# Four source tiles instead of two come row by row at register addresses

## The chip, the cores and the metric

The kernel runs on one core of a Trainium2 chip. The metric is the time of one execution on the device, in microseconds (us). Engines are named as in the profile: PE is TensorE (matmuls), DVE is VectorE, ACT is ScalarE, POOL is GpSimd and SP is SyncE. An engine's instruction queue issues DMAs in order with its other instructions; "ACTq" and "SPq" in a row are such issues.

## The reference

Two graph layers with a residual and a layer norm each, over 3125 nodes of 128 features and 53125 edges that are sorted by destination. Every edge needs the row of x of its source node.

```python
def layer0(h, src, dst, etype, norm, weight, w_comp, bias):
    hsrc, coef = h[src], w_comp[etype]
    msg = sum(hsrc @ weight[b] * coef[:, b][:, None] for b in range(8)) * norm
    return relu(segment_sum(msg, dst, num_segments=h.shape[0]) + bias)

def layer1(node, edge, src, dst, eps, W1, b1, gamma, beta, W2, b2):
    neigh = segment_sum(node[src] + edge, dst, num_segments=node.shape[0])
    h = ((1.0 + eps[0]) * node + neigh) @ W1 + b1
    h = (h - h.mean(0)) * rsqrt(h.var(0) + 1e-5) * gamma + beta
    return relu(h) @ W2 + b2

x = layernorm(x + layer0(x, src, dst, edge_type, edge_weight, ...))
out = layernorm(x + layer1(x, edge_attr, src, dst, ...))
```

## The kernel before

The edges are cut into 416 tiles of 128. Two tiles make a unit (208 units, U), four units a group (52, GROUPS), two units a couple. The main loop goes over the units. For each tile PE multiplies the 128 source rows of x with a one-hot matrix of the destinations that is weighted with the edge's coefficients, and DVE adds the windows that come out into `sums`. As the edges are sorted, the sums of low nodes are complete early; seven parts of the nodes (LOOPED) are therefore finished inside the loop: PE multiplies a part with the bases (line 1339), ACT keeps the result (`keep_agg`, line 1030), PE turns it, DVE makes the layer norm's statistics, ACT takes the deviations (`chunk_deviations`, line 1044), PE turns the normed rows and ACT copies them (`keep_x1_columns`, line 1052). The second layer's neighbour sums run on finished parts as "runs" between the units (line 1374). All of that is an order written out by hand: each engine goes through its own list of units and does a step at the unit where it stands, and semaphores tie the lists together.

The source rows come in three ways.

- POOL gathers a tile with one indirect DMA (`gather_unit`, line 921), up to 16 units ahead of PE (22 early on): 413 tiles.
- SP brings tile 414 (`load_rows_of_tile`, lines 803 to 810). In each of its steps from 23 on (a step is a group) it loads five node numbers from memory into registers (line 805) and issues one DMA of one row of 512 bytes for each (line 809). The five rows of the last tile, 415, it brings in the same way near the end (line 791).
- ACT brings tile 413 (`load_scalar_rows`, lines 1067 to 1074). From unit 152 on, it loads three numbers a unit (line 1069) and issues three row DMAs (line 1073). From there on ACT has no copies of counts left to do (line 1016), but the steps `keep_agg`, `chunk_deviations` and `keep_x1_columns` of the last parts stand between these rows in its queue.

The rows of SP and ACT land in `sums[:, 0, ...]`, in columns of parts whose sums are no longer needed. PE waits for a gathered tile by `gather_in`, for SP's rows by `rows_in` and for ACT's by `etype_rows_in`, in the unit that reads them:

```python
if u * UNIT < ROWED:
    pe.wait_ge(gather_in[u % RU], landed(u))
else:
    pe.wait_ge(rows_in, 16 * (6 + P + FRESH))
if (u + 1) * UNIT == ROWED:
    pe.wait_ge(etype_rows_in, 16 * (5 + P))
```

After unit 207 come the late bases (line 1348), the last runs and the dense layers, and SP stores the output. `late_bases(0)` stands behind unit 202 and waits for the last copy of `keep_x1_columns` (`x1_kept`).

Of the kernel before, what the change touches and what calls it, by code (L numbers as in the profile page):

```python
# [8 lines left out]
I32 = mybir.dt.int32  # L9
# [6 lines left out]
P = 128  # L16
# [5 lines left out]
UNIT = 2  # L22
# [4 lines left out]
ROW_STEP = 22  # L27
ROWS_EACH = 5
SCALAR_UNIT = 152
SCALAR_EACH = 3  # L30
PAIR = 2
# [11 lines left out]
def gnn_resnorm_kernel(nc, x, src, dst, edge_attr, etype, norm, weight, w_comp, bias0,  # L43
# [11 lines left out]
    N, F = x.shape  # L55
# [6 lines left out]
    T = -(-E // P)  # L62
# [51 lines left out]
    TWINS = 3  # L114
    ROWED = T - 2
    assert ROWED * P + P + FRESH == E and ROWED % UNIT == 0
    COUNT_FASTER = 2 * RING * GROUP
# [164 lines left out]
    with ExitStack() as ctx:  # L282
# [89 lines left out]

        row_place, row_sources = sums[:, 0, 0:F], sums[0:1, 0, F:2 * F].bitcast(I32)

        scalar_place, scalar_sources = sums[:, 0, 2 * F:3 * F], sums[0:1, 0, 3 * F:4 * F].bitcast(I32)

        def gathered_tile(t):

            if ROWED <= t < T - 1:
                return row_place  # L380
            if t == ROWED - 1:
                return scalar_place
            first = RING * GROUP
            if first <= t < first + SPARE:
                return sums[:, 0, SPARE_AT + (t - first) * F:SPARE_AT + (t - first + 1) * F]
            return gathered[:, (t if t < first else t - SPARE) % first, :]
# [290 lines left out]
        def landed(u):  # L677

            return (u // RU + 1) * 16 * UNIT - (16 if (u + 1) * UNIT == ROWED else 0)

# [11 lines left out]
        def _(sp):  # L692
# [32 lines left out]
            with sp.If(wide < 1):  # L725
# [73 lines left out]
                def load_row_sources():  # L799
                    sp.wait_ge(st_var, PART_AT[2])  # L800
                    sp.dma_start(row_sources, src[ROWED * P:ROWED * P + P].rearrange("(t e) -> t e", t=1)).then_inc(rows_in, 16)

                def load_rows_of_tile(first, last):
                    sp.wait_ge(rows_in, 16 * 6)
                    rows = nc.values_load_multi_w_load_instructions(
                        row_sources[:, first:last], engines=(ENGINE.SP,), min_val=0, max_val=N - 1,
                        skip_runtime_bounds_check_because="sources are node numbers")[1]
                    for i, row in enumerate(rows):
                        sp.dma_start(row_place[first + i:first + i + 1, :],
                                     x[bass.ds(row, 1), :]).then_inc(rows_in, 16)  # L810

                load_attrs(0)
                load_attrs(1)
                for g in range(GROUPS):
# [10 lines left out]
                    if g == ROW_STEP:  # L825
                        load_row_sources()
                    if 0 <= (g - ROW_STEP - 1) * ROWS_EACH < P:
                        at = (g - ROW_STEP - 1) * ROWS_EACH
                        load_rows_of_tile(at, min(P, at + ROWS_EACH))
                    if g == GROUPS - 3:  # L830
                        load_last_rows()
                load_late_rows_of_x()
                sp.wait_ge(gather_in[(U - 2) % RU], landed(U - 2))
                for b in LOAD_ORDER[12:13] + LOAD_ORDER[6:12]:
# [53 lines left out]
        def _(pool):  # L888
# [19 lines left out]
            def gather_unit(u):  # L908
# [5 lines left out]
                for t in range(u * UNIT, (u + 1) * UNIT):  # L914
                    if u >= FLYING + RU:
                        pool.wait_ge(tiles_read, t - RU * UNIT + 1)
                    elif u >= FLYING:
                        pool.wait_ge(tiles_read, t - FLYING * UNIT + 1)
                    if t + 1 >= ROWED:
                        continue  # L920
                    pool.indirect_dma_start(  # L921
                        gathered_tile(t), None, x[:, :],
                        bass.IndirectOffsetOnAxis((src_slots if t < AHEAD else src_i)[:, t:t + 1], 0)).then_inc(gather_in[u % RU], 16)
# [30 lines left out]
        def _(act):  # L954
# [106 lines left out]
            def load_scalar_sources():  # L1061

                first = (ROWED - 1) * P
                act.dma_start(scalar_sources, src[first:first + P].rearrange("(t e) -> t e", t=1)).then_inc(etype_rows_in, 16)

            def load_scalar_rows(first, last):
# [4 lines left out]
                    skip_runtime_bounds_check_because="sources are node numbers")[1]  # L1071
                for i, row in enumerate(rows):
                    act.dma_start(scalar_place[first + i:first + i + 1, :],
                                  x[bass.ds(row, 1), :]).then_inc(etype_rows_in, 16)

            places = [None] * GU
            with act.If(wide < 1):
# [4 lines left out]
                for u in range(U):  # L1082
# [6 lines left out]
                    if u == SCALAR_UNIT - 4:  # L1089
                        load_scalar_sources()  # L1090
                    if 0 <= (u - SCALAR_UNIT) * SCALAR_EACH < P:
                        at = (u - SCALAR_UNIT) * SCALAR_EACH
                        load_scalar_rows(at, min(P, at + SCALAR_EACH))
                    for k in range(LOOPED):
# [94 lines left out]
        def _(pe):  # L1189
# [74 lines left out]
            def narrow_sums():  # L1264
# [46 lines left out]
                def products_of_step(u):  # L1311
# [4 lines left out]
                    if counts:  # L1316
                        twin_product(counts[0])
                        count_product(counts[0], 0)
                    if u * UNIT < ROWED:
                        pe.wait_ge(gather_in[u % RU], landed(u))  # L1320
                    else:
                        pe.wait_ge(rows_in, 16 * (6 + P + FRESH))
                    if (u + 1) * UNIT == ROWED:
                        pe.wait_ge(etype_rows_in, 16 * (5 + P))
                    for i in range(UNIT):
# [805 lines left out]
```

## Time and profile before

| | us |
|---|---|
| median of 3 runs | 592.95 (591.94 to 595.67) |
| profiled execution, its own time | 591.92 |
| its span, from first to last instruction | 590.1 |
| PE busy | 499.6 |
| DVE busy | 464.3 |
| POOL busy | 399.0 |
| ACT busy | 220.3 |

Busy time counts an engine's work on data. The issue of a DMA, a load of registers and a wait on a semaphore are not in it, so a queue can be full while its engine's share is low. "Idle before" of a group of instructions is the time in which the engine did nothing ahead of them, and the arrow names what ended it. The granted clock is TensorE's, as a share of 2.4 GHz.

### The profile page before, as it was taken

The numbers are of one execution on the slowest core, as the hardware profiler recorded it, in microseconds if no ns is written. First come the engines' busy times: TensorE is split into PE (matmuls) and PEld (weight loads), VectorE is DVE, ScalarE is ACT, GpSimd is POOL, SyncE is SP. The second block draws the span as 40 slices with busy tenths as digits, with TensorE's granted clock in tenths as the row PEclk, the third lists the DMA queues.
The fourth block names the chain that finished last, engine by engine and source line by source line (L and its number), as shares of the span: only waits on it lengthen the run. The fifth ranks groups of instructions, "written<-read, shape, count | busy, mean of one in ns | idle before, by whom it ended". The sixth has DMA issues, their size and how long they took to land. (4 is left out here: it accounts for less than half of the span.)

```text
span 590.1 us, 13829 instructions
## 1 busy us (share of the span) xinstructions
PE 499.6 (85%) x3981; PEld 422.8 (72%) x3981; DVE 464.3 (79%) x1835; ACT 220.3 (37%) x325; POOL 399.0 (68%) x431
## 2 busy tenths in 40 slices
PE   3679887997977977878986888988999797798995
PEld 2458787876866766757575676677989787797675
DVE  5999999989998699989789888895554655655476
ACT  8914446445343264434354442430000000003386
POOL 7777777777777777777777777777777777750000
PEclk9987779597687898989889999999999978989999
DMA  5423757565676395667675775887575765743003
GB/s 142 126 51 90 249 186 220 174 200 180 201 242 238 87 308 161 217 216 245 206 228 189 227 258 189 269 278 226 182 243 141 230 197 154 227 121 119 2 1 109
DMA packets 103807, 108.18 MB, mean 183 GB/s; under 512 B 11726, under 2 KB 90822, under 8 KB 103730
## 3 DMA queue, kind: packets, MB, share of 16 engines
q1 hardware_dynamic: 84286, 77.88, 40.5%
q0 software_dynamic: 13216, 27.09, 17.1%
q10 hardware_dynamic: 6228, 2.30, 1.5%
q8 instruction: 34, 0.56, 0.4%
q14 instruction: 43, 0.35, 0.2%
HBM read 81.67 MB, written 25.56 MB: 182 GB/s over the span
## 5 line engine op out<-in xcount | busy, mean ns | idle before, releaser
L921 POOL DMA_INDIRECT gathered_flat<-in_x_dram,src_i x399 | 382.8, 959 | 121.6 <-issue 89.3
L1016 ACT ACTIVATE adj_flat<-psum 128x500 f16<-128x500 f32 (+1 forms) x208 | 127.4, 612 | 193.1 <-PE psum L1302 185.4
L1278 PE MATMUL psum<-weighted,gathered_flat 128*128 128x96 f32 (+1 forms) x804 | 142.8, 305 | 27.1 <-DMA gathered_flat<-in_x_dram,src_i 27.0
L1271 PEld LDWEIGHTS psum<-hot,attrs 128*128 128x128 f32 x832 | 146.5, 214 | 12.4 <-issue 9.7
L1278 PEld LDWEIGHTS psum<-weighted,gathered_flat 128*128 128x128 f32 x804 | 122.3, 213 | 30.9 <-DMA gathered_flat<-in_x_dram,src_i 30.7
L1782 DVE TENSOR_SCALAR etype_hot<-iota_key,key_t 128x300 f16<-128x300 f16 (+1 forms) x416 | 135.3, 327 | 0.0
L1271 PE MATMUL psum<-hot,attrs 128*128 128x12 f32 (+1 forms) x832 | 132.4, 236 | 2.4 <-DVE weighted L1663 2.4
L1302 PE MATMUL psum<-etype_hot 128*128 128x300 f16 (+1 forms) x416 | 128.0, 345 | 3.4 <-DVE etype_hot L1782 3.3
L1779 DVE TENSOR_SCALAR etype_hot<-iota_key,gathered_flat 128x128 f16<-128x128 f16 x416 | 106.8, 257 | 15.2 <-issue 8.7
L1911 DVE TENSOR_TENSOR sums_flat<-psum,sums_flat 128x180 f32 x208 | 71.2, 342 | 26.1 <-DVE sums_flat L1859 4.8
L1859 DVE TENSOR_TENSOR sums_flat<-psum,sums_flat 128x132 f32 x160 | 45.8, 293 | 52.6 <-PE psum L1374 23.5
L1374 PE MATMUL psum<-sums_flat 128*128 128x264 f16 x552 | 69.4, 279 | 6.6 <-DVE weighted L1663 6.5
L1374 PEld LDWEIGHTS psum<-sums_flat 128*128 128x128 bf16 x552 | 54.0, 101 | 17.4 <-issue 8.4
L1302 PEld LDWEIGHTS psum<-etype_hot 128*128 128x128 f16 x416 | 54.5, 141 | 7.8 <-DVE etype_hot L1782 4.3
L1663 DVE TENSOR_TENSOR weighted<-hot,psum 128x384 f32<-128x384 f32 x104 | 58.2, 601 | 1.8
L1374 PE MATMUL psum<-coef,sums_flat 128*128 128x264 f16 x366 | 52.2, 294 | 3.3 <-DVE weighted L1663 3.3
L1297 PE MATMUL psum<-twin_hot,etype_hot 128*128 128x25 f16 x182 | 35.3, 194 | 19.3 <-DVE etype_hot L1782 17.7
L1297 PEld LDWEIGHTS psum<-twin_hot,etype_hot 128*128 128x128 f16 x182 | 28.9, 159 | 28.1 <-DVE etype_hot L1782 26.0
L1374 PEld LDWEIGHTS psum<-coef,sums_flat 128*128 128x128 bf16 x366 | 37.9, 107 | 13.1 <-issue 5.2
L1339 PE MATMUL psum<-sums_flat,gathered_flat 128*128 128x512 f32 (+1 forms) x112 | 45.6, 542 | 0.5 <-DVE sums_flat L1859 0.5
L1339 PEld LDWEIGHTS psum<-sums_flat,gathered_flat 128*128 128x128 f32 x112 | 22.3, 206 | 10.8 <-issue 9.5
L997 ACT ACTIVATE adj_flat<-zero_col 128x900 f16<-128x900 f32 (+1 forms) x26 | 25.0, 962 | 11.8 <-DVE coef L1640 11.8
(168 smaller groups left out, 390.2 us busy)
## 6 DMA issues: line engine op xcount, KB each, us to landing
attrs<-in_edge_attr_dram SPq DMA_DIRECT2D x51, 512.0 KB
adjacency<-adj_flat SPq DMA_DIRECT2D x26, 900.0 KB
coef<-adjacency SPq DMA_DIRECT2D x24, 288.0 KB, 4.7
gathered_flat<-in_x_dram,src_i POOLq DMA_INDIRECT x399
sums_flat<-adjacency SPq DMA_DIRECT2D x10, 576.0 KB
sums_flat<-adjacency SPq DMA_DIRECT2D x10, 288.0 KB
sums_flat<-adjacency SPq DMA_DIRECT2D x6, 360.0 KB, 5.8
sums_flat<-in_x_dram SPq DMA_DIRECT2D x128, 0.5 KB
```

Source lines behind the costliest of these rows:

```text
L921: pool.indirect_dma_start(gathered_tile(t), None, x[:, :], bass.IndirectOffsetOnAxis((src_slots if t < AHEAD else src_i)[:, t:t + 1], 0)). ...
L1016: nc.scalar.activation(window, counts, ACT.Copy).then_inc(counts_copied, 1)
L1271: product = nc.tensor.matmul(last_row(u, i), attrs[:, s * GROUP + j, :], hot_tiles(s, i)[:, u % GU, :], start=(u % 2 == 0 and i == 0), sto ...
L1278: nc.tensor.matmul(unit_psum(u)[:, 0:B, STARTS[i]:STARTS[i] + WIDTHS[i]], gathered_tile(u * UNIT + i), weighted_tiles(u // GU % 2, i)[:, u ...
L1297: nc.tensor.matmul(adj_counts(c)[:, :, 0:1], low_hot[:, (c - 1) % KEYRING, UNIT - 1, :], twin_hot[:, (c - 1) % (TWINS * GU), :].unsqueeze( ...
L1302: product = nc.tensor.matmul(adj_counts(c)[:, :, STARTS[i]:STARTS[i] + WIDTHS[i]], low_hot[:, c % KEYRING, i, :], key_hot[:, c % KEYRING, ...
L1339: product = nc.tensor.matmul(psum[:, chunk_bank(k), 0:n], w_base[:, b, :], sums[:, b, lo:lo + n], start=(b == 0), stop=(b == B - 1))
L1374: product = nc.tensor.matmul(psum[:, bank, 0:BLOCK * SPAN], x1_part(k, c)[:, i * F:(i + 1) * F], counts[:, :, 0:SPAN], start=(opens and h ...
L1663: last = nc.vector.tensor_tensor(weighted_tiles(s % 2, i), hot_tiles(s % 2, i).unsqueeze(2).to_broadcast([P, HALF, B, n]), shown_coef(g % ...
L1779: nc.vector.tensor_scalar(low_hot[:, u % KEYRING, i, :], iota_key[:, 0:P], low_t[:, t:t + 1], None, ALU.is_equal)
L1782: last = nc.vector.tensor_scalar(key_hot[:, u % KEYRING, i, 0:n], iota_key[:, 0:n], key_t[:, t:t + 1], None, ALU.is_equal)
L1911: nc.vector.tensor_tensor(window, unit_psum(u), window, ALU.add).then_inc(added, 1)
```

## The change

Tiles 411 to 414 come row by row now, two by ACT (411 and 412) and two by SP (413 and 414). POOL gathers 411 tiles. SP loads ten numbers a step instead of five and issues ten rows, in the same steps 23 to 48. ACT loads five numbers a unit instead of three and issues five rows, from unit 152 on as before; that takes 52 units (152 to 203) where it took 43 (152 to 194). The second tile of each counts on a semaphore of its own (`src_in`, `norm_in`), and PE waits for them in units 205, 206 and 207.

```diff
-ROWS_EACH = 5
+ROWS_EACH = 10
 SCALAR_UNIT = 152
-SCALAR_EACH = 3
+SCALAR_EACH = 5
...
-    ROWED = T - 2
+    ROWED, SCALARED = T - 3, T - 5
...
-        row_place, row_sources = sums[:, 0, 0:F], sums[0:1, 0, F:2 * F].bitcast(I32)
-
-        scalar_place, scalar_sources = sums[:, 0, 2 * F:3 * F], sums[0:1, 0, 3 * F:4 * F].bitcast(I32)
+        def dead_sums(k, at, n):
+
+            return sums[:, 0, PARTS[k][0] + at * F:PARTS[k][0] + (at + n) * F]
+        row_sources, scalar_sources = (dead_sums(k, 2, 2)[0:1, :].bitcast(I32) for k in range(2))
...
-                    for i, row in enumerate(rows):
-                        sp.dma_start(row_place[first + i:first + i + 1, :],
-                                     x[bass.ds(row, 1), :]).then_inc(rows_in, 16)
+                    for i, row in enumerate(rows, first):
+                        sp.dma_start(gathered_tile(ROWED + i // P)[i % P:i % P + 1, :],
+                                     x[bass.ds(row, 1), :]).then_inc((rows_in, src_in)[i // P], 16)
...
-                sp.wait_ge(gather_in[(U - 2) % RU], landed(U - 2))
+                sp.wait_ge(gather_in[(U - 3) % RU], landed(U - 3))
...
-                    if t + 1 >= ROWED:
+                    if t >= SCALARED:
                         continue
...
-                    if 0 <= (u - SCALAR_UNIT) * SCALAR_EACH < P:
+                    if 0 <= (u - SCALAR_UNIT) * SCALAR_EACH < 2 * P:
                         at = (u - SCALAR_UNIT) * SCALAR_EACH
-                        load_scalar_rows(at, min(P, at + SCALAR_EACH))
+                        load_scalar_rows(at, min(2 * P, at + SCALAR_EACH))
...
-                    if u * UNIT < ROWED:
+                    if u * UNIT < SCALARED:
                         pe.wait_ge(gather_in[u % RU], landed(u))
-                    else:
+                    if u == U - 3:
+                        pe.wait_ge(etype_rows_in, 16 * (5 + P))
+                    if u == U - 2:
+                        pe.wait_ge(norm_in, 16 * (4 + P))
                         pe.wait_ge(rows_in, 16 * (6 + P + FRESH))
-                    if (u + 1) * UNIT == ROWED:
-                        pe.wait_ge(etype_rows_in, 16 * (5 + P))
+                    if u == U - 1:
+                        pe.wait_ge(src_in, 16 * (4 + P))
```

On ACT, at the end of its part of the main loop. TENSOR_LOAD fetches the node numbers, each ISA with the DMA behind it is one row, L1044 and L1052 (L1053 after) are the last part's deviations and copy, L1037 (L1038) is the first late part. Before:

```order
L1069 TENSOR_LOAD sums_flat
L1073 ISA
L1073 DMA sums_flat<-in_x_dram 1x128
L1073 ISA
L1073 DMA sums_flat<-in_x_dram 1x128
L1044 ACTIVATE ln_std<-ln_mv,ln_eps_col 128x2
L1052 ACTIVATE sums_flat<-psum 128x256
L1037 ACTIVATE sums_flat<-psum,bias_col 128x160
```

And now, where five rows stand behind the first load and one behind the second:

```order
L1074 DMA sums_flat<-in_x_dram 1x128
L1053 ACTIVATE sums_flat<-psum 128x256
L1070 TENSOR_LOAD sums_flat
L1074 ISA
L1074 DMA sums_flat<-in_x_dram 1x128
...
L1070 TENSOR_LOAD sums_flat
L1074 ISA
L1074 DMA sums_flat<-in_x_dram 1x128
L1038 ACTIVATE sums_flat<-psum,bias_col 128x160
```

The last row was issued ahead of the last part's deviations; now the part's copy stands in the middle of the rows, and the last row is the last thing ahead of the late part.

On PE, units 205 to 207 with their waits. `gather_in` is a gather's semaphore; the first L1278 (L1279) of a unit is its first tile. Before:

```order
L1278 MATMUL psum<-weighted,gathered_flat 128x8x12 [waits gather_in13]
L1278 MATMUL psum<-weighted,gathered_flat 128x8x15
L1271 MATMUL psum<-hot,attrs 128x15
L1271 MATMUL psum<-hot,attrs 128x12 [waits added]
L1278 MATMUL psum<-weighted,gathered_flat 128x8x12 [waits etype_rows_in,gather_in14]
L1278 MATMUL psum<-weighted,sums_flat 128x8x15
L1271 MATMUL psum<-hot,attrs 128x15
L1271 MATMUL psum<-hot,attrs 128x12
L1278 MATMUL psum<-weighted,sums_flat 128x8x12 [waits rows_in]
```

And now:

```order
L1279 MATMUL psum<-weighted,gathered_flat 128x8x12 [waits etype_rows_in,gather_in13]
L1279 MATMUL psum<-weighted,sums_flat 128x8x15
L1272 MATMUL psum<-hot,attrs 128x15
L1272 MATMUL psum<-hot,attrs 128x12 [waits added]
L1279 MATMUL psum<-weighted,sums_flat 128x8x12 [waits rows_in,norm_in]
L1279 MATMUL psum<-weighted,sums_flat 128x8x15
L1272 MATMUL psum<-hot,attrs 128x15
L1272 MATMUL psum<-hot,attrs 128x12
L1279 MATMUL psum<-weighted,sums_flat 128x8x12 [waits src_in]
```

The products are the same; unit 206 no longer waits for a gather but for all rows of ACT (`norm_in`) and SP's first tile, and the last gather is unit 205's.

## Rows read from the trace of the kernel before

**Rows 1.** The page: span, busy times, digits of ACT and POOL in 40 slices.

```profile
span 590.1 us, 13829 instructions
...
PE 499.6 (85%) x3981; PEld 422.8 (72%) x3981; DVE 464.3 (79%) x1835; ACT 220.3 (37%) x325; POOL 399.0 (68%) x431
...
ACT  8914446445343264434354442430000000003386
POOL 7777777777777777777777777777777777750000
```

**Rows 2.** The page's costliest groups: POOL's gathers (busy, mean ns | idle before).

```profile
L921 POOL DMA_INDIRECT gathered_flat<-in_x_dram,src_i x399 | 382.8, 959 | 121.6 <-issue 89.3
```

**Rows 3.** The timeline of POOL: its last two gathers (start us, us).

```profile
524.53 0.94 POOL L921 DMA_INDIRECT gathered_flat<-in_x_dram,src_i  x1 [0.30 <-issue]
525.78 0.94 POOL L921 DMA_INDIRECT gathered_flat<-in_x_dram,src_i  x1 [0.30 <-issue]
```

**Rows 4.** The timeline of PE: unit 190, late bases, unit 206.

```profile
493.00 1.21 PE L1278 MATMUL psum<-weighted,gathered_flat 128*128 128x96 f32 x4 [2.96 <-DMA gathered_flat<-in_x_dram,src_i]
...
523.48 2.33 PE L1348 MATMUL psum<-sums_flat,gathered_flat 128*128 128x160 f32 x16
...
529.33 0.46 PE L1278 MATMUL psum<-weighted,gathered_flat 128*128 128x96 f32 x2
```

**Rows 5.** The timeline of ACT and its queue from 396 on.

```profile
397.19 3.86 ACTq L1073 DMA_DIRECT2D sums_flat<-in_x_dram  x6
...
437.69 21.08 ACTq L1073 DMA_DIRECT2D sums_flat<-in_x_dram  x27
458.82 0.47 ACT L1030 ACTIVATE sums_flat<-psum,bias_col 128x256 f32<-128x256 f32 x1 [21.87 <-DMA sums_flat<-in_x_dram]
459.95 6.12 ACTq L1073 DMA_DIRECT2D sums_flat<-in_x_dram  x9
...
467.61 13.44 ACTq L1073 DMA_DIRECT2D sums_flat<-in_x_dram  x18
...
500.63 0.47 ACT L1030 ACTIVATE sums_flat<-psum,bias_col 128x256 f32<-128x256 f32 x1 [19.14 <-PE psum L1339]
...
519.66 0.39 ACT L1052 ACTIVATE sums_flat<-psum 128x256 f32<-128x256 f32 x1 [13.20 <-PE psum L1363]
```

**Rows 6.** The same: one batch of three rows, and the last batch, of two.

```profile
447.40 1.25 ACTq L1073 DMA_DIRECT2D sums_flat<-in_x_dram  x3
...
503.88 0.88 ACTq L1073 DMA_DIRECT2D sums_flat<-in_x_dram  x2
```

**Rows 7.** The timeline of SP's queue: one step's five rows.

```profile
452.66 1.96 SPq L809 DMA_DIRECT2D sums_flat<-in_x_dram  x5
```

**Rows 8.** Waits of SP's queue (us in total, times, longest): attribute loads, for PE.

```profile
SPq L731 <- PE psum L1271: 299.9, 49, 30.5
```

**Rows 9.** Register loads by line and stretch (ns min/median/max, first and last start).

```profile
L1069 ACTq TENSOR_LOAD <-sums_flat x41: 879/978/1964, 395.1 to 496.0; - x41
L1069 ACTq TENSOR_LOAD <-sums_flat x1: 760/760/760, 503.0 to 503.0; - x1
L805 SPq TENSOR_LOAD <-sums_flat x26: 695/1252/1302, 254.3 to 509.3; - x26
L805 SPq TENSOR_LOAD <-sums_flat x1: 712/712/712, 298.1 to 298.1; - x1
L805 SPq TENSOR_LOAD <-sums_flat x3: 1252/1254/1264, 305.7 to 328.6; - x3
L805 SPq TENSOR_LOAD <-sums_flat x1: 848/848/848, 509.3 to 509.3; - x1
L1005 ACTq TENSOR_LOAD <-base_row x52: 305/309/1088, 42.7 to 389.6; - x52
```

**Rows 10.** DMA queues from 505.8 to 506.5: ACT's (packets, MB, share).

```profile
q10 hardware_dynamic: 8, 0.00, 1.3%
```

**Rows 11.** Busy times by stretch, behind a wait of PE (PEclk 0.58).

```profile
493.00:497.00 4.00, 4.00 (x14) 3.56 (x15) 0.59 (x2) 0.00 (x0) 2.84 (x3) 0.58 0.20 55
```

More of the change, by code:

```diff
@@ L114, in gnn_resnorm_kernel @@
     TWINS = 3
-    ROWED = T - 2
-    assert ROWED * P + P + FRESH == E and ROWED % UNIT == 0
+    ROWED, SCALARED = T - 3, T - 5
+    assert (T - 1) * P + FRESH == E and (SCALARED - 1) % UNIT == 0
     COUNT_FASTER = 2 * RING * GROUP
@@ L371, in gnn_resnorm_kernel @@
         gathered = gathered_flat[:, 0:RING * GROUP * F].rearrange("p (t f) -> p t f", f=F)
-        row_place, row_sources = sums[:, 0, 0:F], sums[0:1, 0, F:2 * F].bitcast(I32)
-        scalar_place, scalar_sources = sums[:, 0, 2 * F:3 * F], sums[0:1, 0, 3 * F:4 * F].bitcast(I32)
+        def dead_sums(k, at, n):
+            return sums[:, 0, PARTS[k][0] + at * F:PARTS[k][0] + (at + n) * F]
+        row_sources, scalar_sources = (dead_sums(k, 2, 2)[0:1, :].bitcast(I32) for k in range(2))
         def gathered_tile(t):
             if ROWED <= t < T - 1:
-                return row_place
-            if t == ROWED - 1:
-                return scalar_place
+                return dead_sums(0, t - ROWED, 1)
+            if SCALARED <= t < ROWED:
+                return dead_sums(1, t - SCALARED, 1)
             first = RING * GROUP
@@ L677, in landed @@
         def landed(u):
-            return (u // RU + 1) * 16 * UNIT - (16 if (u + 1) * UNIT == ROWED else 0)
+            return (u // RU + 1) * 16 * UNIT - (16 if (u + 1) * UNIT - 1 == SCALARED else 0)
         def tiles_of(n):
@@ L800, in load_row_sources, with load_rows_of_tiles @@
                     sp.wait_ge(st_var, PART_AT[2])
-                    sp.dma_start(row_sources, src[ROWED * P:ROWED * P + P].rearrange("(t e) -> t e", t=1)).then_inc(rows_in, 16)
-                def load_rows_of_tile(first, last):
+                    sp.dma_start(row_sources, src[ROWED * P:(ROWED + 2) * P].rearrange("(t e) -> t e", t=1)).then_inc(rows_in, 16)
+                def load_rows_of_tiles(first, last):
                     sp.wait_ge(rows_in, 16 * 6)
@@ L826, in _ @@
                         load_row_sources()
-                    if 0 <= (g - ROW_STEP - 1) * ROWS_EACH < P:
+                    if 0 <= (g - ROW_STEP - 1) * ROWS_EACH < 2 * P:
                         at = (g - ROW_STEP - 1) * ROWS_EACH
-                        load_rows_of_tile(at, min(P, at + ROWS_EACH))
+                        load_rows_of_tiles(at, min(2 * P, at + ROWS_EACH))
                     if g == GROUPS - 3:
@@ L1061, in load_scalar_sources @@
             def load_scalar_sources():
-                first = (ROWED - 1) * P
-                act.dma_start(scalar_sources, src[first:first + P].rearrange("(t e) -> t e", t=1)).then_inc(etype_rows_in, 16)
+                act.dma_start(scalar_sources, src[SCALARED * P:(SCALARED + 2) * P]
+                              .rearrange("(t e) -> t e", t=1)).then_inc(etype_rows_in, 16)
             def load_scalar_rows(first, last):
@@ L1071, in load_scalar_rows @@
                     skip_runtime_bounds_check_because="sources are node numbers")[1]
-                for i, row in enumerate(rows):
-                    act.dma_start(scalar_place[first + i:first + i + 1, :],
-                                  x[bass.ds(row, 1), :]).then_inc(etype_rows_in, 16)
+                for i, row in enumerate(rows, first):
+                    act.dma_start(gathered_tile(SCALARED + i // P)[i % P:i % P + 1, :],
+                                  x[bass.ds(row, 1), :]).then_inc((etype_rows_in, norm_in)[i // P], 16)
             places = [None] * GU
```

## The prediction

> **What bounds the kernel now.** I read the page first, then the timelines of GpSimd (POOL), TensorE (PE) and ScalarE (ACT) over the last third, then the single instructions of ACT and SyncE (SP) that the change multiplies.
>
> PE is the busiest engine at 85% [rows 1], but it is not what paces the main loop: POOL's line of digits is a flat 7 up to the last gathers, with no slice that differs [rows 1]. A gather takes 0.94 us and the next starts 1.25 us after it [rows 3], and its idle time is its own issue, not a wait: 89.3 of 121.6 us [rows 2]. Two gathers make a unit, so POOL paces the loop at 2.5 us a unit. PE meets that pace: 3 us of waiting for a gather before 493.00 [rows 4]. The last gather starts at 525.78 [rows 3], and the unit that needs it (206) begins its products at 529.33 [rows 4]. Everything after that, 60.8 us to the end of the span at 590.1, hangs on it.
>
> So gathers are worth removing, and their price is plain. The question is who does the work instead. ACT's digits say it is idle in the last third [rows 1], but those count its arithmetic alone. The timeline that shows its queue says otherwise: from 397.19 it issues rows with hardly a pause (27 rows in 21.08 us are one piece of it), and the steps that stand between the rows start only when the rows ahead of them are out: the part kept at 458.82 has the row DMAs as what ended its idle time, not PE [rows 5]. Only at 500.63 does ACT wait for PE again, and at 519.66 for 13.20 us [rows 5]. ACT's spare time is thus little more than the 20-odd us behind its last row at 504.76 [rows 6]. The change needs 128 more rows.
>
> **The change part by part.**
>
> *Two gathers fewer on POOL:* 2 x 1.25 = 2.50 us earlier for the last gather [rows 3], if nothing else is late.
>
> *SP: ten rows a step.* Five rows take 1.96 us of SP's queue [rows 7], so five more are 2.0 us, and its load of ten row numbers up to 1.0 us more than five by the prices below. SP then waits for PE before the next attribute load: 299.9 us in 49 waits, 6.1 us each [rows 8]. That wait hides it; such a load is for a group two ahead, so even where a wait is shorter, a load one or two us late has a whole group's time to spare. Taken at nothing; at most 1 us if that cover is gone.
>
> *ACT: 256 rows in 52 batches of five, where 43 batches of three stood.* Both start at unit 152 behind the last copy of counts, so the first row stays at 397.19 [rows 5]. Now the price of a batch.
>
> A batch of three: 27 rows took 21.08 us from first to last, 9 rows took 6.12 [rows 5], so six batches are 14.96 us, 2.49 us for one; 18 rows in 13.44 [rows 5] give 7.32 for three batches, 2.44 for one. I take 2.47. A row more: 1.25 us for three rows against 0.88 for two [rows 6], 0.39 with the rounding of the longer stretch. Two rows more are 0.78.
>
> The rest of a batch is the load of row numbers into registers, and it grows too. On ACT it takes 0.978 us for three numbers and 0.760 for two [rows 9], 0.22 a number. On SP it takes 0.848 us for three and 1.252 for five at the median [rows 9], 0.20 a number. But not always: four numbers from a table whose groups of four are aligned cost ACT 0.309, and some of SP's loads of five cost about 0.70: one at 298.1, and behind it three dear ones before 338 [rows 9]. SP's loads stand at places 0, 5, 10, and so on in their list, and the cheap ones are every fourth: those whose place is a multiple of four. I take it that four numbers at such a place go in one piece. ACT's new loads stand at the same places. So a cheap load on ACT is SP's least, 0.70, with the 0.13 by which ACT's load of three exceeds SP's: 0.83. A dear one is 1.252 + 0.13 = 1.38.
>
> A dear batch is 2.47 + 0.78 + (1.38 - 0.98) = 3.65 us, a cheap one 2.47 + 0.78 - 0.15 = 3.10. From the first row of the first batch to the first row of the 51st lie 50 of them, 38 dear and 12 cheap: 138.7 + 37.2 = 175.9 us. Then the rows of that batch, 1.25 + 0.78 = 2.03, and the last one with one number and one row, 0.78 + 0.49. Two loads of x between the rows cost 0.3 each: 467.61 comes 1.54 us after the rows before it end, where 1.22 is usual [rows 5]. The last row is issued by 397.19 + 175.9 + 2.03 + 1.27 + 0.6 = **577.0**, against 504.76 now. The last rows moved by 506.5, 1.7 us behind their issue [rows 10], so they land by 578.7. PE waits for all of them before unit 206.
>
> PE's own way there: the copy at line 1052, 519.66 now, stands behind the 50th batch: 397.19 + 172.3 + 2.03 + 0.6 = 572.1, done at 572.5. PE's late products (523.48 now) wait for it, and from there to unit 206 were 5.85 us [rows 4], so 578.3 at full clock. PE will have idled, and after the 3 us of waiting before 493.00 the granted clock was 0.58 over 4 us [rows 11], mostly the lower of its two levels, 1.2 GHz, which cost 4 x 0.42 = 1.7 us. So 580.0, and that is the later of the two. On the way ACT leads at every other meeting: the part kept at 458.82 now falls at about 484 and PE needs it before it can go on, VectorE (DVE) the same for the deviations. The loop is paced by ACT at 3.5 us a unit, POOL and DVE wait behind it, and POOL's 2.50 us are worth nothing.
>
> The sum: unit 206 goes from 529.33 to 580.0, **+50.7 us**; the 60.8 us behind it stay. Span 590.1 + 50.7 = 640.8. The profiled execution was 591.92, 1.8 us outside its span, and the median of the runs is 1.03 above it: 643.6, rounded to 643.5.
>
> The bounds. From below: a load costs 0.98 whatever it holds, so all batches are 3.25: 50 x 3.25 = 162.5, 13.4 us less, 630. From above: no load is cheap, 50 x 3.65 = 182.5, 6.6 us more, 650. I take the middle value because the cheap and dear loads of five on SP are the same form at the same places.
>
> On that price the Trainium skill has a rule. "Runtime: NRT & Kernel Launch", section "Instruction fetch mechanics", says that loading registers costs some 200 ns for each, in bulk too. The trace agrees with it for three against two numbers (0.22) and not for four in 0.309 us; by the rule the sum would be the upper bound, 650.
>
> **The rivals.**
>
> *ACT keeps up: not slower.* The rows are issued in time and PE gets the last gather 2.50 us earlier: 592.95 - 2.5 = 590.5. The point that decides is the price of a batch. Unit 206 stays where it is if ACT's last row is out by 527.6, that is (527.6 - 397.19 - 3.9) / 50 = 2.53 us a batch, and the full gain needs 2.48. A batch of three already costs 2.47. For it speaks that ACT has 13 us of idle time before 519.66 and that four numbers can load in 0.309: with that price a batch of five is 2.47 + 0.78 - 0.67 = 2.58, and the time 592.95 + 50 x 0.05 = 595.5. Against it: none of ACT's loads from this table came near that; the shortest with three numbers, 0.879 [rows 9], would still give 2.47 + 0.78 - 0.10 = 3.15. Chance 5%, nearly all of it within 1% of before.
>
> The Trainium skill speaks for this rival: "DMA: Bandwidth & Descriptors", section "Issuing engines are not separate DMA queues", says that issuing on several engines saves only the issuing sequencer's time, usually small beside the transfer. Here a row of 512 bytes costs ACT 0.8 us with its share of the load, so the trace of this case is against it.
>
> *A flat price for a load:* 630, as worked out. For it: no run shows five numbers on ACT. Chance 18%.
>
> *Every load dear:* 650. For it: the one aligned load on ACT that is cheap reads another table, written by VectorE. Chance 10%.
>
> *It doesn't do what it says.* The order of instructions shows 52 loads with five rows each and PE's wait for them ahead of unit 206, so 1% at most; 593.
>
> **How the numbers follow.** The forecast has 64%, the flat price 18%, every load dear 10%, ACT in time or no change 6%, and 2% go to something that I don't see. The range 628 to 651 holds the first three with a us or two around the bounds, about 9 in 10; narrower would cut off a bound. The runs before lie 3.7 us apart, 0.6%, so 1% (5.9 us) is about what a measurement can tell from no change. Faster by over 1%: 1%. Within 1%: 5%. Slower by over 1%: 94%.
>
> **What would show it.** In the profile after: ACT's row issue from 397 to about 577 in pieces of 5 rows each 3.1 or 3.65 us apart, its loads at two prices (about 0.83 and 1.38); the copy at the old line 1052 near 572; waits of PE, PEld and DVE on ACT in the last third, tens of us where there is next to nothing now; POOL's pace above 2.5 us a unit from about 415 on; unit 206 near 580 and some 61 us behind it. I am wrong if ACT's batches come out under 2.6 us, if the loop up to 395 changes by more than 2 us (then SP's ten rows matter), or if the time behind unit 206 grows.

## The result, and the profile after

The kernel after takes 645.02 us (median; 643.31 to 646.68), the kernel before 593.87 on the same chip: a ratio of 1.0851, with a 95% interval of 1.0805 to 1.0898. The profiled execution took 643.84 us, 1.7 of it outside its span.

The page of the kernel after answers to [rows 1].

```profile
span 642.1 us, 14605 instructions
...
PE 509.6 (79%) x3981; PEld 430.6 (67%) x3981; DVE 465.2 (72%) x1835; ACT 220.2 (34%) x325; POOL 395.5 (62%) x429
```

Busy times hardly differ from before, but the span is 52 us longer. Only PE's busy time and that of its weight loads (PEld) grow, by 10 and 8 us, at a mean granted clock of 0.876 against 0.909. So most of the 52 us is not dearer work; engines wait. ACT's own 220 us, the smallest of the five, say nothing of it, since issues of DMAs and register loads don't count as busy. The timeline of ACT and its queue, which answers to [rows 5], shows where the time went (start, us; the bracket is the idle time before and what ended it).

```profile
394.31 7.44 ACTq L1074 DMA_DIRECT2D sums_flat<-in_x_dram  x10
...
453.24 30.30 ACTq L1074 DMA_DIRECT2D sums_flat<-in_x_dram  x45
483.59 0.47 ACT L1031 ACTIVATE sums_flat<-psum,bias_col 128x256 f32<-128x256 f32 x1 [30.93 <-DMA sums_flat<-in_x_dram]
...
517.25 22.93 ACTq L1074 DMA_DIRECT2D sums_flat<-in_x_dram  x35
540.24 0.47 ACT L1031 ACTIVATE sums_flat<-psum,bias_col 128x256 f32<-128x256 f32 x1 [24.19 <-issue]
...
552.08 19.87 ACTq L1074 DMA_DIRECT2D sums_flat<-in_x_dram  x30
572.00 0.38 ACT L1053 ACTIVATE sums_flat<-psum 128x256 f32<-128x256 f32 x1 [20.60 <-issue]
573.54 3.25 ACTq L1074 DMA_DIRECT2D sums_flat<-in_x_dram  x6
```

Rows are issued from 394.31 to 576.79 with no pause but their loads and ACT's own steps, and each of the three steps shown comes as soon as the rows ahead of it are out: the part kept at 458.82 before is kept at 483.59, the one at 500.63 at 540.24, and the copy at 519.66 (now line 1053) at 572.00. Before, PE ended two of these three waits; now the queue itself ends them.

The register loads of ACT answer to [rows 9] (ns min/median/max, first and last start): all 52, and one stretch.

```profile
L1070 ACTq TENSOR_LOAD <-sums_flat x52: 554/1394/1877, 393.4 to 575.6; - x52
L1070 ACTq TENSOR_LOAD <-sums_flat x1: 783/783/783, 452.3 to 452.3; - x1
L1070 ACTq TENSOR_LOAD <-sums_flat x9: 808/1392/1446, 455.3 to 483.6; - x9
```

The load at 452.3, at place 80 of the list, is one of the cheap ones; they come every fourth, at 0.72 to 0.89 us, and between them stand the dear ones, near 1.40. The least of the list, 0.554, is the last load, of one number.

Who waits for it is in the table of waits (us in total, times, longest). Waits on these lines are not among the largest of the kernel before.

```profile
PEld psum L1359 <- ACT sums_flat L1031: 27.4, 6, 13.9
...
DVE sums_flat L1800 <- PE psum L1359: 26.4, 3, 13.4
PE psum L1359 <- ACT sums_flat L1031: 26.2, 5, 13.8
```

The timeline of PE after answers to [rows 4]: the products behind the copy, units 203 and 206.

```profile
572.53 4.60 PE L1352 MATMUL psum<-sums_flat,gathered_flat 128*128 128x160 f32 x16 [8.48 <-ACT sums_flat L1053]
...
577.21 1.19 PE L1279 MATMUL psum<-weighted,gathered_flat 128*128 128x96 f32 x4
...
581.18 0.68 PE L1279 MATMUL psum<-weighted,sums_flat 128*128 128x96 f32 x4
```

The sixteen products that took 2.33 us [rows 4] take 4.60: PE had idled for 8.48 us before them, and the granted clock, in the table of stretches that answers to [rows 11] (length, busy of PE, PEld, DVE, ACT, POOL, then PEclk), is 0.58, mostly the lower level of 1.2 GHz.

```profile
572.00:580.00 8.00, 7.47 (x38) 7.37 (x38) 1.03 (x3) 0.78 (x2) 0.00 (x0) 0.58 0.02 4
```

Unit 206 begins at 581.18, 51.85 us later than before, and the 60.9 us behind it are the 60.8 of before. That is the whole difference.

One line answers to [rows 3], and it is not what I expected: the last gather on the timeline of POOL.

```profile
522.46 0.94 POOL L922 DMA_INDIRECT gathered_flat<-in_x_dram,src_i  x1 [0.30 <-issue]
```

It is tile 410's, and it starts 0.8 us earlier than the same gather before (525.78 less two of 1.25 is 523.28). PE fell far behind, and POOL did not slow down.

### The profile page after: what moved, and what is told of

It is laid out like the page before. It is cut to its first block and busy times, and to the rows that moved or that the text cites. A ratio compares the mean times of both kernels' runs of the same rounds, so it can differ in the third digit from the quotient of the medians.

```text
span 642.1 us, 14605 instructions
## 1 busy us (share of the span) xinstructions
PE 509.6 (79%) x3981; PEld 430.6 (67%) x3981; DVE 465.2 (72%) x1835; ACT 220.2 (34%) x325; POOL 395.5 (62%) x429
## 5 line engine op out<-in xcount | busy, mean ns | idle before, releaser
L1279 PE MATMUL psum<-weighted,gathered_flat 128*128 128x96 f32 (+1 forms) x800 | 143.3, 307 | 18.9 <-DMA gathered_flat<-in_x_dram,src_i 18.8
L1279 PEld LDWEIGHTS psum<-weighted,gathered_flat 128*128 128x128 f32 x800 | 123.1, 216 | 21.9 <-DMA gathered_flat<-in_x_dram,src_i 21.8
L1303 PE MATMUL psum<-etype_hot 128*128 128x300 f16 (+1 forms) x416 | 125.8, 341 | 2.9 <-DVE etype_hot L1786 2.7
L1783 DVE TENSOR_SCALAR etype_hot<-iota_key,gathered_flat 128x128 f16<-128x128 f16 x416 | 105.5, 254 | 11.2 <-PE psum L1303 5.6
L1378 PE MATMUL psum<-sums_flat 128*128 128x264 f16 x552 | 71.5, 284 | 6.2 <-DVE weighted L1667 5.5
L1378 PE MATMUL psum<-coef,sums_flat 128*128 128x264 f16 x366 | 55.4, 306 | 14.3 <-DVE sums_flat L1863 9.8
L1343 PE MATMUL psum<-sums_flat,gathered_flat 128*128 128x512 f32 (+1 forms) x112 | 47.9, 566 | 6.8 <-DVE sums_flat L1915 6.8
L1343 PEld LDWEIGHTS psum<-sums_flat,gathered_flat 128*128 128x128 f32 x112 | 23.6, 218 | 17.5 <-issue 8.5
L1053 ACT ACTIVATE sums_flat<-psum 128x512 f32<-128x512 f32 (+2 forms) x9 | 4.1, 456 | 78.1 <-issue 41.5
```

The lines of the kernel that those rows point to most:

```text
L1279: nc.tensor.matmul(unit_psum(u)[:, 0:B, STARTS[i]:STARTS[i] + WIDTHS[i]], gathered_tile(u * UNIT + i), weighted_tiles(u // GU % 2, i)[:, u ...
L1303: product = nc.tensor.matmul(adj_counts(c)[:, :, STARTS[i]:STARTS[i] + WIDTHS[i]], low_hot[:, c % KEYRING, i, :], key_hot[:, c % KEYRING, ...
L1343: product = nc.tensor.matmul(psum[:, chunk_bank(k), 0:n], w_base[:, b, :], sums[:, b, lo:lo + n], start=(b == 0), stop=(b == B - 1))
L1378: product = nc.tensor.matmul(psum[:, bank, 0:BLOCK * SPAN], x1_part(k, c)[:, i * F:(i + 1) * F], counts[:, :, 0:SPAN], start=(opens and h ...
L1783: nc.vector.tensor_scalar(low_hot[:, u % KEYRING, i, :], iota_key[:, 0:P], low_t[:, t:t + 1], None, ALU.is_equal)
```

## The experiments

**Halves.** The first two kernels do one half of the change each, on one chip with the two kernels behind them. The edits here are against the kernel after, unless the text says otherwise, and are shown in part.

```diff
-ROWED, SCALARED = T - 3, T - 5     # SyncE 2, ScalarE 2 tiles
+ROWED, SCALARED = T - 3, T - 4     # SyncE's half: ScalarE 1 tile,
+SCALAR_EACH = 3                    #   three rows a unit
+ROWED, SCALARED = T - 2, T - 4     # ScalarE's half: SyncE 1 tile,
+ROWS_EACH = 5                      #   five rows a step
...
```

> SyncE's half of the change alone: SyncE brings two tiles at ten rows a step, ScalarE one tile at three rows a unit as before, 412 gathers. My theory (ScalarE's in-order queue is the whole loss, SyncE's ten rows are free): one gather fewer is worth 1.25 us, so 592.6 against 593.9, ratio 0.998, and no wait of PE on ScalarE of more than a few us. Rival (SyncE's longer steps make attribute loads and stores late): slower than before, 595 to 600, with PE or DVE waiting for SyncE's DMAs.

> ScalarE's half alone: ScalarE brings two tiles at five rows a unit, SyncE one tile at five rows a step as before, 412 gathers. My theory: 645, within 1.5 us of the whole change, because ScalarE's last row is again out near 577. Rival (SyncE's ten rows carry part of the loss): 640 or less, and the missing part in the kernel with SyncE's half alone.

SyncE's half: 593.64 us, ratio 0.9971 (0.9947 to 0.9995). ScalarE's half: 644.82, ratio 1.0854 (1.0812 to 1.0897). So the loss is ACT's alone, to within the measurement. In the trace of SyncE's half, SP's 26 loads take what two prices say, 1.13 for ten numbers at a place that is a multiple of four and 2.26 at the others, but for one of 3.25 and the last, of six numbers (the whole list, then one of each):

```profile
L806 SPq TENSOR_LOAD <-sums_flat x26: 1119/1326/3251, 254.9 to 507.9; - x26
L806 SPq TENSOR_LOAD <-sums_flat x1: 1127/1127/1127, 399.3 to 399.3; - x1
L806 SPq TENSOR_LOAD <-sums_flat x1: 2267/2267/2267, 408.4 to 408.4; - x1
```

The dear one is 1 us more than five at the dear price, as the prediction had it, and it cost nothing. The interval of this half even lies just below 1, as one gather fewer at 1.25 us would give; the kernels with more gathers fewer, further down, don't repeat it.

**Fewer loads, the same rows.**

```diff
-if 0 <= (u - SCALAR_UNIT) * SCALAR_EACH < 2 * P:                       # 5 a unit
+if (u - SCALAR_UNIT) % 3 == 0 and 0 <= (u - SCALAR_UNIT) // 3 * 16 < 2 * P:  # 16 every third
...
```

> The whole change, but ScalarE loads sixteen row numbers at a time, at places that are multiples of sixteen, every third unit: 16 loads in place of 52, the same 256 rows. My theory (four aligned numbers load in one piece): a load of sixteen takes 0.9 to 1.4 us, a batch 16 x 0.39 + 1.2 = 7.4 us or a little more, 16 batches 118 to 125 us, the last row out at 513 to 522, and the time 591 to 596. Rival (each register costs 0.2 us whatever its place): a load takes 3.5 us, a batch 10 us, the last row is out near 557, and the time is 622 to 632. Rival (the rows, not the loads, are what is dear): over 632.

599.74 us, ratio 1.0085 (1.0055 to 1.0114). The sixteen loads of sixteen numbers and their first and last rows:

```profile
L1070 ACTq TENSOR_LOAD <-sums_flat x16: 1195/1286/1361, 396.6 to 518.2; - x16
```

```profile
397.96 7.72 ACTq L1074 DMA_DIRECT2D sums_flat<-in_x_dram  x16
...
519.65 6.33 ACTq L1074 DMA_DIRECT2D sums_flat<-in_x_dram  x16
```

Sixteen numbers cost less than five at a place that is no multiple of four (1.29 against 1.40), and 45 of the 51 us are gone with the rows untouched: per-register pricing falls. The time is 4 us above what I gave, and the trace shows two things behind that. The batch is dearer: from 397.96 to 519.65 lie 15 of them, 8.1 us each where I had 7.4. And ACT's copies still stand behind stretches of up to 48 rows, so that PE reaches unit 206 at 537, not 529.

**What the gathers are worth.** In the next kernel ScalarE brings one tile at three rows a unit again, only 411 tiles are gathered, and nobody brings tile 412: PE reads the rows of tile 411 a second time. The one after it drops nine gathers more, and PE reads what stands in their places.

```diff
-return dead_sums(1, t - SCALARED, 1)
+return dead_sums(1, 0, 1)          # tile 412 not brought
-ROWED, SCALARED = T - 3, T - 5
+ROWED, SCALARED, LEFT_OUT = T - 3, T - 5, T - 14   # second kernel: tiles 402 to 410 neither
...
```

> What two gathers are worth without any row for them: SyncE brings two tiles at ten rows a step, ScalarE one at three rows a unit as before, 411 gathers; tile 412 is not brought at all, and PE reads the rows of tile 411 twice (that part of the computation is left out). My theory (POOL paces the loop, 1.25 us a gather): the last gather starts 2.5 us earlier and the time is 591.4, ratio 0.996. Rival (PE or the late copies set the end already, so the gathers are worth nothing): 593.9, ratio 1.000.

> The kernel of the run before, in which tile 412 is left out, with nine more gathers left out: tiles 402 to 410 are not gathered either, PE reads what stands in their places (that part of the computation is left out), 402 gathers in all. New theory after the kernel without tile 412 gained nothing: behind 515 PE waits for no gather any more, its own products and the lower granted clock set unit 206, so the time stays within 2 us of 593.5, ratio 0.995 to 1.001. Rival, the reading of the prediction (POOL's last gather sets unit 206): 11 x 1.25 = 13.8 us less than before, 581, ratio 0.977.

Without tile 412: 593.58 us, ratio 0.9995 (0.9971 to 1.0019); the 2.5 us that I expected (0.996) lie just outside. With nine gathers fewer still: 594.33, ratio 1.0005 (0.9982 to 1.0028), where the prediction's reading wanted 0.977. The trace of the second shows POOL's last gather long before the end, and PE without a wait for one from 514.03 on.

```profile
512.22 1.09 POOL L922 DMA_INDIRECT gathered_flat<-in_x_dram,src_i  x1 [0.30 <-issue]
```

```profile
512.05 0.70 PE L1279 MATMUL psum<-weighted,gathered_flat 128*128 128x96 f32 x4 [2.03 <-DMA gathered_flat<-in_x_dram,src_i]
...
514.03 1.21 PE L1279 MATMUL psum<-weighted,gathered_flat 128*128 128x96 f32 x4 [0.92 <-DMA gathered_flat<-in_x_dram,src_i]
...
531.89 0.68 PE L1279 MATMUL psum<-weighted,sums_flat 128*128 128x96 f32 x4
```

The last gather lies 20 us ahead of unit 206 (531.89), and the time is the same. So in this kernel the last gathers do not set the end. What PE does instead is in the table of stretches of that kernel: behind its waits it is busy without a pause, with a granted clock of 0.50, the lower level, from 515 to 525.

```profile
515.00:520.00 5.00, 5.00 (x27) 4.25 (x26) 3.46 (x11) 0.38 (x1) 0.00 (x0) 0.50 0.56 176
520.00:525.00 5.00, 5.00 (x27) 4.45 (x27) 2.47 (x8) 0.00 (x0) 0.00 (x0) 0.50 0.01 3
```

The kernel before has the same order: its last wait for a gather ends at 514.82, PE is then busy without a pause, and the row of unit 206 in [rows 4] has no idle time ahead of it. Only the clock is back sooner, at 0.97 from 520 to 525.

```profile
514.82 1.21 PE L1278 MATMUL psum<-weighted,gathered_flat 128*128 128x96 f32 x4 [2.09 <-DMA gathered_flat<-in_x_dram,src_i]
```

```profile
515.00:520.00 5.00, 5.00 (x25) 4.46 (x26) 3.46 (x12) 0.34 (x1) 3.78 (x5) 0.50 0.54 152
520.00:525.00 5.00, 5.00 (x45) 4.70 (x44) 2.38 (x8) 0.05 (x1) 3.78 (x5) 0.97 0.43 132
```

These two kernels drop the last gathers alone. None of the runs makes POOL faster ahead of 515, where PE does wait for it, so what that would be worth isn't shown.

**Lighter products.** That asks for a test of PE's own work: two products where six stood, in the runs from unit 198 on, once without tile 412 and once in the kernel before. That leaves out two of the three parts of x1 in these runs.

```diff
-block_products(run_bank(n), tiles_in(run_buffer(n), first, first, last))
+block_products(run_bank(n), tiles_in(run_buffer(n), first, first, last),
+               parts=(2,) if RUNS[n][0] >= 198 else (0, 1, 2))
...
```

> The kernel that leaves out tile 412 (411 gathers), with less work for PE behind 511: the six products of a run at unit 198 and later are two (only the third of three parts of x1 is taken), which leaves that part of the computation out too. My theory (PE's own products at the lower clock set unit 206 there): four products fewer at 0.21 us in each of four units and at 0.11 in a fifth take 3.5 to 4 us off, 590, ratio 0.993 to 0.995. Rival (a transfer sets it): no change to that kernel, ratio 0.999 to 1.000.

> The kernel before with 413 gathers and the same lighter products at unit 198 and later (the same part of the computation is left out). My theory: PE now waits for the last gathers again, so that most of what it saves is lost and the two gathers fewer of the other kernel are worth their 2.5 us here: 592.5 to 594, ratio 0.997 to 1.000, 2 to 2.5 us above the kernel with 411 gathers and light products. Rival (the gathers don't decide here either): the same time as that kernel within 1 us.

594.73 us, ratio 1.0015 (0.9992 to 1.0039), and 595.01, ratio 1.0006 (0.9986 to 1.0027). Both theories fail: no gain, and no difference between the two, as the second one's rival had it. The timelines of PE show where it stays. Without tile 412, unit 206 and the last bases, and the stretch of the last bases (clock 1.00):

```profile
533.28 0.68 PE L1279 MATMUL psum<-weighted,sums_flat 128*128 128x96 f32 x4
...
536.36 2.29 PE L1351 MATMUL psum<-sums_flat,gathered_flat 128*128 128x149 f32 x16 [1.37 <-DVE sums_flat L1914]
```

```profile
536.30:538.70 2.40, 2.29 (x16) 2.07 (x16) 0.01 (x1) 0.01 (x1) 0.00 (x0) 1.00 0.90 255
```

The same with the lighter products (clock 0.50):

```profile
522.07 1.21 PE L1279 MATMUL psum<-weighted,gathered_flat 128*128 128x96 f32 x4 [0.26 <-DMA gathered_flat<-in_x_dram,src_i]
...
529.97 0.69 PE L1279 MATMUL psum<-weighted,sums_flat 128*128 128x96 f32 x4
...
533.52 4.34 PE L1351 MATMUL psum<-sums_flat,gathered_flat 128*128 128x149 f32 x16 [1.84 <-DVE sums_flat L1914]
538.34 0.90 PE L1358 MATMUL psum<-ident,sums_flat 128*128 128x128 f32 x3 [0.48 <-ACT sums_flat L1038]
```

```profile
533.50:538.00 4.50, 4.34 (x16) 3.98 (x16) 0.00 (x0) 0.10 (x1) 0.00 (x0) 0.50 0.72 225
```

Unit 206 comes 3.3 us earlier, much as expected, but the spans are 594.2 and 593.8. Behind it the sixteen products run at the lower level, 2.05 us longer, the wait for DVE grows by 0.47, and the next two groups lose another 0.6 (the transposes 0.90 against 0.55, the group behind them 4.49 against 4.21). With the lighter products PE also meets a gather again, at 522.07, for 0.26 us. In this pair, what was saved ahead of unit 206 was given back behind it at the lower clock. That the saving caused the fall isn't shown: SyncE's half, with all its products, has the same wait as the first of the pair, and the same sixteen products at 3.71 us.

```profile
532.60 3.71 PE L1350 MATMUL psum<-sums_flat,gathered_flat 128*128 128x149 f32 x16 [1.38 <-DVE sums_flat L1913]
```

All of that is read from one execution of each; the four ratios say only that none of these cuts is worth what a measurement can tell.

**Loads doubled.** In the kernel before, each load of three numbers is issued twice. In a first version the second load's numbers replaced the first's, in the mended one the rows are taken by turns from both (load stands for the call that loads registers).

```diff
-rows = load(scalar_sources[:, first:last])
+for _ in range(2):                                      # first version
+    rows = load(scalar_sources[:, first:last])
+a, b = (load(scalar_sources[:, first:last]) for _ in range(2))   # mended
+rows = [(a, b)[i % 2][i] for i in range(last - first)]
```

> The kernel before, with one thing doubled: ScalarE loads each three row numbers twice, and issues the same 128 rows. My theory (a load holds ScalarE's queue for 0.98 us, and the queue decides as soon as a batch is dearer than 2.53 us): a batch is 2.47 + 0.98 = 3.45 us, the 43rd begins at 397.2 + 42 x 3.45 = 542, the copy behind the rows comes at 544, unit 206 at 550 to 553, and the time is 609 to 617. Rival (the rows alone are what holds the queue, a load passes beside them): 594.

> The kernel before, with ScalarE's loads of row numbers really doubled: the kernel with a second load of the same numbers ran 43 loads, not 86, so that its second load was dropped on the way to the chip and it was a repetition of the kernel before. Here each batch loads its three numbers twice and takes its rows by turns from the one and the other, so that neither can be dropped. My theory (a load holds ScalarE's queue for 0.98 us, and the queue decides as soon as a batch is dearer than 2.53 us): 3.45 us a batch, the 43rd begins near 542, unit 206 at 550 to 553, and the time is 609 to 617. Rival (a load passes beside the rows): 594.

The first version measured 593.12, ratio 0.9983 (0.9958 to 1.0007), and its trace holds 43 loads, not 86: the unused one was dropped, so it tests nothing of the loads. But it is the kernel before once more, with the same 13829 instructions, and its profiled execution has a span of 593.5 us, 3.4 longer: PE stays at the lower level from 520 to 525, where the kernel before had 0.97, and unit 206 begins at 532.51 instead of 529.33.

```profile
520.00:525.00 5.00, 5.00 (x27) 4.52 (x26) 2.41 (x7) 0.00 (x0) 3.77 (x4) 0.50 0.40 125
```

So two executions of one program can lie as far apart, by the clock behind PE's waits, as the single traces that were compared above. The mended version has 86 and takes 619.75 us, ratio 1.0416 (1.0367 to 1.0465). The same 128 rows, a load more for each batch, 25 us. Its loads, and the timeline of ACT:

```profile
L1069 ACTq TENSOR_LOAD <-sums_flat x86: 487/750/2226, 395.8 to 532.3; - x86
```

```profile
450.19 26.73 ACTq L1074 DMA_DIRECT2D sums_flat<-in_x_dram  x27
476.97 0.47 ACT L1030 ACTIVATE sums_flat<-psum,bias_col 128x256 f32<-128x256 f32 x1 [28.27 <-DMA sums_flat<-in_x_dram]
...
528.34 0.47 ACT L1030 ACTIVATE sums_flat<-psum,bias_col 128x256 f32<-128x256 f32 x1 [21.82 <-DMA sums_flat<-in_x_dram]
```

The timeline of PE:

```profile
528.87 0.69 PE L1356 MATMUL psum<-ident,sums_flat 128*128 128x128 f32 x2 [8.29 <-ACT sums_flat L1030]
```

27 rows take 26.73 us where they took 21.08 [rows 5]: 5.65 over the eight pairs of loads inside, 0.71 for a second load and not 0.98, or 3.18 a batch. Still the time is 2.8 us above what I gave, because I priced the wrong meeting. It was the part kept at 528.34, against 500.63 [rows 5], that held PE, which had idled for 8.29 us: 27.7 us late, and the span is 27.7 us longer (617.8 against 590.1).

**Where the rows go instead.** The same four tiles and 411 gathers, but SyncE brings three.

```diff
-ROWS_EACH, SCALAR_EACH = 10, 5
-ROWED, SCALARED = T - 3, T - 5
+ROWS_EACH, SCALAR_EACH = 16, 3      # third tile: its own place and sources
+ROWED, SCALARED = T - 4, T - 5
...
```

> The same four tiles by rows and the same 411 gathers as the change, divided otherwise: SyncE brings three of them, sixteen rows a step at places that are multiples of sixteen, ScalarE one at three rows a unit as before. My theory (the loss is ScalarE's queue alone, and SyncE has the idle time): the whole loss of 50 us is gone, 593 to 595, ratio 0.998 to 1.003; no gain, since two gathers were worth nothing in the kernel that left a tile out. Rival (rows at register addresses cost as much on SyncE, whose loads and stores come late): 600 and more.

603.64 us, ratio 1.0174 (1.0144 to 1.0204): 41 of the 51 us are gone, but not all, and the rival is right about the rest. The table of waits of SP's queue, the page's chain by line, and two steps' rows:

```profile
SPq L733 <- PE psum L1283: 185.9, 28, 30.6
```

```profile
SPq L819 10%; PE psum L1389 5%; SPq L769 2%; SPq L815 2%; PE psum L1544 2%; PE psum L1290 1%; PE psum L1567 1%; DMA sums_flat<-in_x_dram 1%; PE psum L1558 1%; PE psum L1283 1%; DMA adjacency<-adj_flat 1%; SPq L733 1%; PE psum L1363 1%; DMA attrs<-in_edge_attr_dram 1%; DVE sums_flat L1926 0%
```

```profile
464.28 6.49 SPq L819 DMA_DIRECT2D sums_flat<-in_x_dram  x16
...
474.59 6.45 SPq L819 DMA_DIRECT2D sums_flat<-in_x_dram  x16
```

Sixteen rows take 6.5 us and their load 1.2. With SP's other issues a step comes to 10.3 us here, where four units of 2.5 leave 10. The 49 waits of [rows 8] are 28, so nearly half the steps have none left, SP's rows are in the chain that ended last, and PE waits for attribute loads, 10.1 us in six waits (table of waits), where no such wait stands among those of the kernel before; the span is 10.5 us longer.

```profile
PE psum L1283 <- DMA attrs<-in_edge_attr_dram: 10.1, 6, 4.0
```

**Aligned loads with SyncE's half**, for a version that might beat both.

```diff
-ROWS_EACH, SCALAR_EACH = 10, 3
+ROWS_EACH, SCALAR_EACH = 12, 4
...
```

> The kernel with SyncE's half alone, all loads at places that are multiples of four: SyncE twelve rows a step, ScalarE four a unit in 32 batches. My theory: a load of four takes ScalarE 0.3 to 0.55 us and a batch 1.9 to 2.2, its last row is out near 475, and this is worth nothing more, since nothing waited for ScalarE there: ratio to before 0.996 to 0.999, as with SyncE's half alone. Rival (ScalarE's copies, late behind rows, still cost something in the kernel before): 590 or less, ratio under 0.994.

592.23 us, ratio 0.9989 (0.9963 to 1.0015). Loads of four take ACT 0.58 us, and its last row is out near 480 instead of 505, each a little above what I gave:

```profile
L1070 ACTq TENSOR_LOAD <-sums_flat x32: 480/580/653, 394.7 to 477.8; - x32
```

```profile
471.26 8.98 ACTq L1074 DMA_DIRECT2D sums_flat<-in_x_dram  x16
```

Nothing waited for ACT, so nothing is gained. No version here beats the kernel before by 1%; SyncE's half, 0.3% below it, comes nearest.

**Copies or rows.** The last question is which of ACT's two ways to unit 206 is the later one.

```diff
-gathered_tile(u * UNIT + i)
+gathered_tile(ROWED if SCALARED <= u * UNIT + i < ROWED else u * UNIT + i)
-if u == U - 3: pe.wait_ge(etype_rows_in, 16 * (5 + P))   # and norm_in at U - 2
+# both waits stand behind narrow_sums()
...
```

> The whole change, ScalarE issuing all 256 rows as there, but nobody waiting for them before the products behind unit 207 are out: PE reads SyncE's first tile in place of tiles 411 and 412 (that part of the computation is left out). It tells the two ways apart by which ScalarE's queue can reach unit 206: its own copies, which stand in order behind the rows, or the rows themselves. My theory (the copies are the later of the two): 643 to 646, ratio 1.083 to 1.088, as with the whole change. Rival (the last rows): 5 us and more below it.

646.45 us, ratio 1.0874 (1.0844 to 1.0905), no less than the whole change. PE waits for the copy as in the kernel after, with no row of ACT's to wait for.

```profile
573.38 4.61 PE L1349 MATMUL psum<-sums_flat,gathered_flat 128*128 128x160 f32 x16 [8.72 <-ACT sums_flat L1053]
```

## Why the prediction was right, point by point

*ACT's batch.* Held. Loads at places that are multiples of four took about 0.80 us (forecast 0.83), the others 1.40 (1.38), and both halves of the change confirm that ACT carries the whole loss. The two rivals on the load's price fall: a flat price, since loads run from 0.55 for one number to 1.40 for five, and every load dear, since every fourth was cheap and sixteen numbers took 1.29. The Trainium skill, "Runtime: NRT & Kernel Launch", section "Instruction fetch mechanics", has some 200 ns a register in bulk too. The runs agree at places that are no multiple of four, where five numbers cost 0.42 us more than three, and not at aligned ones, where sixteen numbers cost 0.08 us each.

*The sum along the queue.* The first row came 2.9 us earlier than taken (394.31), and the batches cost 2.7 us more between them: 573.54 - 394.31 is 179.2 where 175.9 and 0.6 for the loads of x were set. The two cancelled, so that the copy at 572.00 (forecast 572.1) and the last row at 576.8 (577.0) are closer than the terms deserve; that is luck. Of the 2.9 us, 1.2 are the first load, 0.73 us instead of 1.96. The rest touches a sign of being wrong, a loop up to 395 that changes by more than 2 us: ACT's last copy of counts comes at 390.37 instead of 392.79. But that is earlier, not later, and in the kernels with SyncE's ten rows it lies anywhere from 390.37 to 394.51, so the sign was set within what single traces scatter by.

*PE's own way is the later of the two.* Held, by the kernel that doesn't wait for the rows. The term for the cold clock was too small: from the products at the copy to unit 206 took 8.65 us, against 5.85 at full clock, so 2.8 and not 1.7. Unit 206 was 1.2 us later than forecast, and the span 1.3.

*SP's ten rows at nothing.* Held at ten; the kernel with sixteen shows how near the bound was. A mean wait of 6.1 us a step is not spare time in every step.

*POOL's pace above 2.5 us a unit.* Wrong. POOL went on at its own pace to 522.46 while PE, which waited for ACT, was at unit 191 at 525 when the last gather, of unit 205, was out: the places for tiles absorbed it.

*Two gathers are worth 2.50 us, and everything behind the last gather hangs on it.* Wrong, in the part on what bounds the kernel. Eleven gathers fewer changed nothing that can be measured. In the trace of before, too, PE waits for gathers until about 515 and then runs its own products, with no wait ahead of unit 206; that the last gather's landing and PE's arrival at unit 206 lie close together is what I took for cause. The term was set at nothing for another reason, that ACT hides it, so the sum didn't suffer. The rival in which ACT keeps up would have: it promised 590.5, 2.5 us below the kernel before, and the runs show no such gain.

*What stays open:* what sets the end of the kernel before to within 3 us. The runs exclude the last gathers and the products behind unit 198 each by itself and both together, at the clock as it came. How long the lower level lasts behind PE's waits moved unit 206 by 3.2 us between two executions of one program, which is as much as the cuts were to save. But no run changed the clock, and none made POOL faster ahead of 515.

## What to carry to other kernels

Price an engine's queue by everything that it issues, register loads and DMA issues included: an engine at 37% busy had no time left, and each step of its own behind the rows came as late as the rows. Load row numbers many at a time, from places that are multiples of four; here 16 aligned loads of sixteen for 52 of five gave back 45 of 51 us (what the place and what the fewer loads are worth each was not separated). Before counting on fewer instructions of the engine that seems to set the pace, leave some out and see whether the end moves.

## What the runs showed of the hardware

A load of row numbers into registers is priced by place, and the prices fit pieces of four: on ACT 0.58 us for four aligned numbers, 0.80 for five from an aligned place, 1.40 for five from another, 1.29 for sixteen aligned; on SP 0.93 for twelve, 1.13 for ten aligned and 2.26 for ten at a place that is even but no multiple of four. A second load of the same three numbers cost 0.71 us a batch where one alone takes 0.98. A load whose registers nobody reads did not reach the chip: 43 loads stood in the trace where 86 were written. And the same sixteen products behind a wait of PE took from 2.29 us at a granted clock of 1.00 to 4.34 at 0.50, in kernels whose times agree.
